# Channel sums taken from x as loaded, down products scaled into SBUF in one instruction, every offset on GpSimd, and new orders on all engines

## The chip, the cores and the metric

The kernel runs on one core of a Trainium2 chip. The time is device microseconds of one launch; 81.67 us is the median of three runs (81.64 to 82.47). Engines: TensorE (PE), VectorE (DVE), ScalarE (ACT), GpSimd (POOL), and SyncE (SP), which here only issues transfers. Every engine works through its own instructions in the order written and waits on semaphores.

## The reference

The input x is [64 batches, 64 tokens, 256 channels] in fp32, cond is [64, 128]. Two conditioned residual layers are applied:

```python
dg, db, ug, ub = (cond @ t for t in (down_gamma, down_beta, up_gamma, up_beta))
w_down = down_project[None] * dg[:, None] + db[:, None]          # [b, 256, 64]
act = relu(einsum('bsd,bdh->bsh', x, w_down))
w_up = up_project[None] * ug[:, None] + ub[:, None]              # [b, 64, 256]
x = x + (einsum('bsh,bhd->bsd', act, w_up) + x)                  # layer 0
styles = cond @ (affine_w * gain).T + affine_b
dcoefs = rsqrt(sum((weight * styles)**2) + 1e-8)
y = clip(einsum('blc,oc->blo', x * styles, weight) * dcoefs + bias, -256, 256)
x = x + y                                                        # layer 1
```

Since `db` is the same for all channels of one batch and one h, its share of the down product is `db` times the sum of x over the 256 channels of a token: the **channel sum**. Likewise `ub` needs the sum of `act` over h.

## The kernel before

The 4096 tokens are worked in eight tiles of 512 tokens (eight batches). For a tile t the stages are:

1. `transpose_in`: PE turns x (`x_nat`, tokens on partitions) into channels on partitions, in PSUM `ps_io`. ACT copies it to `hT` (`evacuate_x`).
2. `pair_x` (POOL, L582) adds the two halves of 128 channels of `hT` into `x_pair`.
3. `down_project` (PE, L713) and `down_sum` (PE, L720, ones times `x_pair`) fill the two halves of `ps_down`: the product (g=0) and the channel sum spread over all h (g=1). Tokens 0 to 255 lie on partitions 0 to 63, the others on 64 to 127. Tile 1 uses a bank of `ps_y` for this, since `ps_down` holds the result up to `relu_low`.
4. `scale_down` (DVE, L374) multiplies each half by its table, g=1 into SBUF `sum_sc`, g=0 in place in PSUM. `sum_down` (L381) adds them in place in PSUM. `relu_high` (ACT) and `relu_low` (DVE, L386 and L388) write the rounded relu and its rest to `act_hl`.
5. `up` (PE, L733 to L735): up product in `ps_up`, sum over h in `ps_sum`. `scale_up` and `add_up` (DVE, L394 and L407) make `hT` = scaled up product + `hT`. `evacuate_sum` (ACT) copies `ps_sum`; POOL's `offset_scale` (L588) and `offset_add` (L597) add the `ub` share to `hT`. For tile 4 DVE does the scaling itself (`OFFSET_ON_DVE`, L401).
6. `modulate` (POOL, L603): `xm` = `hT` times styles.
7. `linear(t, o)` (PE, L745): the second layer for output half o. Half 0 is demodulated and clipped below on ACT (`demodulate`, 8 instructions, L262), half 1 on DVE (L412, L417) for the tiles of `DEMOD_ON_DVE` and on ACT for tiles 0 and 2. `finish` (DVE, L423) clips above and adds `hT`.
8. `transpose_out` (PE, L699) and `evacuate_out` (ACT, L271), then the store by SP.

The last tile is done in two parts of 256 tokens and two output halves (`end_...`), so that its end is short. Tables (`down_tables`, `up_tables`, `styles`), the transposed weight (`transpose_weight`, L806) and the norms (`norms`, L816, with a root on ACT and one Newton step on DVE) are made in the first 27 us. The order of the work on each engine is a list of calls written out by hand at the end of that engine's block. SP issues all loads first, x tile 0 in four blocks, then tables, tile 1, more tables, the weight, tiles 2 to 7; after that the stores in order, each behind its wait.

Of the kernel before, what the change touches and what calls it, by code (L numbers as in the profile page):

```python
# [5 lines left out]
ALU = mybir.AluOpType  # L6
ACT = mybir.ActivationFunctionType
F32 = mybir.dt.float32
F32R = mybir.dt.float32r

P = 128
# [4 lines left out]
def bass_cond_resid(nc, x, cond, down_project, down_gamma, down_beta, up_project, up_gamma, up_beta,  # L16
# [19 lines left out]
    DEMOD_ON_DVE = (1, 3, 4, 5, 6)  # L36
    OFFSET_ON_DVE = (4,)
# [5 lines left out]
    with ExitStack() as ctx:  # L43
# [42 lines left out]
        sum_sc = sb("sum_sc", [P, HT])  # L86
# [32 lines left out]
        x_paired = sem("x_paired")  # L119
        down_ps, down_scaled, pre_ready = sem("down_ps"), sem("down_scaled"), sem("pre_ready")  # L120
        hi_ready, lo_ready = sem("hi_ready"), sem("lo_ready")
        up_ps, up_scaled, up_added = sem("up_ps"), sem("up_scaled"), sem("up_added")
        act_sum_ready, off_scaled, dve_off_scaled = sem("act_sum_ready"), sem("off_scaled"), sem("dve_off_scaled")
# [18 lines left out]
        def sums_before(t):  # L142

            return sum(n not in OFFSET_ON_DVE for n in range(t))

# [15 lines left out]

        def down_bank(t):

            return ps_y[:, 0].rearrange("p (g t) -> p g t", g=2) if t == 1 else ps_down[:]
# [21 lines left out]
        def _(sp):  # L186
# [13 lines left out]
            def store(n):  # L200
                parts = 1 if n < HALVED else 2
                for part in range(parts):
                    blocks = slice(part * TJ // parts, (part + 1) * TJ // parts)
                    sp.wait_ge(out_ready, outs_before(n) + part + 1)
                    sp.dma_start(out_tiles[n][:, blocks], out_nat[:, n, blocks]).then_inc(out_stored, 16)
# [6 lines left out]
            store(0)  # L212
            store(1)
            store(2)
            store(3)
            store(4)
            store(5)
            end_store(0, 0)
            store(6)
            end_store(0, 1)  # L220
            end_store(1, 0)
            end_store(1, 1)
# [3 lines left out]
        def _(act):  # L226
# [17 lines left out]

            def relu_high(t):
                act.wait_ge(pre_ready, t + 1)
                wait(act, up_ps, t - 1)
                q, pre = t % 2, down_bank(t)[:, 0]
                act.activation(act_hl[0:H, q, 0:HT], pre[0:H], ACT.Relu)
                act.activation(act_hl[H:P, q, HT:T], pre[H:P], ACT.Relu).then_inc(hi_ready, 1)  # L250

            def evacuate_sum(t):
                act.wait_ge(up_ps, t + 1)
                copied = [n for n in range(t) if n not in OFFSET_ON_DVE]
                wait(act, off_scaled, len(copied) - 1)
                act.activation(act_sum[:, len(copied) % 2], ps_sum[:], ACT.Copy).then_inc(act_sum_ready, 1)  # L256
# [70 lines left out]
            evacuate_sum(2)
            relu_high(3)
# [3 lines left out]
            relu_high(4)  # L332
            evacuate_sum(3)
            evacuate_x(6)
            demodulate(1, 0)
            evacuate_x(7)
            relu_high(5)
            demodulate(2, 1)
            demodulate(2, 0)
            evacuate_out(0)  # L340
            relu_high(6)
            evacuate_sum(5)
            evacuate_out(1)
            demodulate(3, 0)
            evacuate_out(2)
            evacuate_sum(6)
            relu_high(7)
            demodulate(4, 0)
            evacuate_out(3)
            evacuate_sum(7)  # L350
            demodulate(5, 0)
            evacuate_out(4)
            demodulate(6, 0)
            evacuate_out(5)
            evacuate_end(0, 0)
            evacuate_out(6)
            evacuate_end(0, 1)
            evacuate_end(1, 0)
            evacuate_end(1, 1)

        @block.vector
        def _(dve):
# [5 lines left out]

            def scale_down(t):
                dve.wait_ge(down_ps, t + 1)  # L370
                wait(dve, pre_ready, t)
                for g, scaled in ((1, sum_sc[:]), (0, down_bank(t)[:, 0])):
                    tab = down_tab[:, t, g].unsqueeze(2).to_broadcast([P, HB, S])
                    last = dve.tensor_tensor(scaled.rearrange("p (b s) -> p b s", s=S),  # L374
                                             down_bank(t)[:, g].rearrange("p (b s) -> p b s", s=S), tab, ALU.mult)
                last.then_inc(down_scaled, 1)

            def sum_down(t):
                dve.wait_ge(down_scaled, t + 1)
                pre = down_bank(t)[:, 0]  # L380
                dve.tensor_tensor(pre, pre, sum_sc[:], ALU.add).then_inc(pre_ready, 1)  # L381

            def relu_low(t):
                dve.wait_ge(hi_ready, t + 1)
                q, pre = t % 2, down_bank(t)[:, 0]
                dve.scalar_tensor_tensor(out=act_hl[H:P, q, 0:HT], in0=pre[0:H], scalar=0.0,  # L386
                                         in1=act_hl[0:H, q, 0:HT].bitcast(F32), op0=ALU.max, op1=ALU.subtract)
                dve.scalar_tensor_tensor(out=act_hl[0:H, q, HT:T], in0=pre[H:P], scalar=0.0,  # L388
# [7 lines left out]

            def offset_scale(t):
                dve.wait_ge(up_ps, t + 1)
                wait(dve, x2_ready, t - 1)
                sums = by_batch(ps_sum[:].unsqueeze(1).to_broadcast([P, DC, T]))  # L400
                dve.tensor_tensor(by_batch(off_sc[:, t % 2]), sums, per_batch(up_tab[:, 1, :, batches(t)]),  # L401
                                  ALU.mult).then_inc(dve_off_scaled, 1)
# [78 lines left out]

            down_tables()
            dve.wait_ge(dtab_sb, 1)
            scale_down(0)
            sum_down(0)
            up_tables()
            relu_low(0)
            scale_down(1)
            sum_down(1)
            dve.wait_ge(utab_sb, 1)  # L490
            scale_up(0)
            relu_low(1)
# [442 lines left out]
```

## Time and profile before

| | |
|---|---|
| three runs, median | 81.67 us |
| profiled execution, its own time | 82.11 us |
| its span | 80.2 us |
| granted TensorE clock | 1.00 (2.4 GHz) throughout |
| busy in the span: PE, DVE, ACT, POOL | 73.5, 60.1, 53.9, 58.9 us |
| loads, stores | 5.15 MB read, 4.19 MB written |

The span runs from the first to the last instruction of the profiled execution; its own time is 1.9 us more. PE being busy 92% doesn't by itself say that it is the limit, because matmuls overlap one another in the records; the chain of waits and the timeline say where nothing but PE stood in the way. A stage in which PE and POOL are both busy all the time has two limits that have to be moved together.

### The profile page before, as it was taken

What the parts mean: (1) busy time and instruction counts of PE and PEld (TensorE: products, weight loads), DVE (VectorE), ACT (ScalarE), POOL (GpSimd) and SP (SyncE); (2) the same over time, 40 slices, a digit from 0 to 9 for tenths busy, and PEclk for the clock granted to TensorE, in tenths of its full rate; (3) what the DMA queues carried; (4) which work ended last, traced back from release to release, by engine and by line L of the source; (5) the groups of instructions that cost most, each with busy time, mean ns of one, the idle gap of its engine ahead of it and who ended that gap; (6) DMA issues with size and microseconds to landing.
All of it is one profiled execution on the core that took longest, in us unless ns stands there. A gap on an engine that the chain in (4) does not pass through costs nothing.

```text
span 80.2 us, 1233 instructions
## 1 busy us (share of the span) xinstructions
PE 73.5 (92%) x378; PEld 45.6 (57%) x378; DVE 60.1 (75%) x105; ACT 53.9 (67%) x131; POOL 58.9 (73%) x41
## 2 busy tenths in 40 slices
PE   4997899998989999999999999999999999999720
PEld 2573586757966536743753564638547464587500
DVE  1001078399799699899799969998999989979820
ACT  0362480876693689974957999569799495297830
POOL 3005360299989999999999999999799999990000
PEclk9999999999999999999999999999999999999999
DMA  1889999996000000000000001542330610702696
GB/s 17 240 222 297 280 272 356 348 349 190 1 0 0 0 0 4 0 0 4 0 0 8 0 0 65 196 167 94 135 126 0 229 36 0 261 0 91 212 328 161
DMA packets 10734, 9.42 MB, mean 117 GB/s; under 512 B 1060, under 2 KB 10728, under 8 KB 10728
## 3 DMA queue, kind: packets, MB, share of 16 engines
q1 hardware_dynamic: 10352, 9.24, 36.6%
q10 hardware_dynamic: 376, 0.10, 0.5%
q8 instruction: 3, 0.05, 0.3%
q14 instruction: 3, 0.02, 0.1%
HBM read 5.15 MB, written 4.19 MB: 116 GB/s over the span
## 4 chain that ended last, share of the span: by engine, by line
PE 76%; DMA 8%; SPq 7%; ACT 2%; DVE 2%; issue 2%
PE ps_y L745 26%; PE ps_io L699 8%; DMA x_nat<-in_x_dram 8%; PE ps_io L688 8%; PE ps_down L713 8%; PE ps_up L733 6%; PE ps_up L734 5%; PE ps_down L720 4%; PE ps_sum L735 2%; PE ps_y L756 2%; PE ps_up L756 2%; PE ps_sum L745 2%; PE ps_down L745 2%; SPq L188 2%; SPq L192 1%
## 5 line engine op out<-in xcount | busy, mean ns | idle before, releaser
L262 ACT ACTIVATE ps_y<-ps_y,vec_cols,demod 128x64 f32<-128x64 f32 x64 | 19.5, 401 | 4.9 <-PE ps_y L745 4.9
L745 PE MATMUL ps_y<-xm,wT 128*128 128x512 f32 x48 | 21.7, 592 | 0.0
L582 POOL TENSOR_TENSOR x_pair<-hT 128x512 f32<-128x512 f32 x8 | 10.2, 1276 | 9.8 <-ACT hT L237 5.4
L597 POOL TENSOR_TENSOR hT<-hT,off_sc 128x1024 f32<-128x1024 f32 x7 | 16.6, 2367 | 0.2
L745 PEld LDWEIGHTS ps_y<-xm,wT 128*128 128x128 f32 x48 | 9.0, 189 | 8.7 <-issue 8.1
L603 POOL TENSOR_TENSOR xm<-hT,style 128x1024 f32<-128x1024 f32 x7 | 13.3, 1904 | 0.3
L588 POOL TENSOR_TENSOR off_sc<-act_sum,up_tab 128x1024 f32<-128x1024 f32 x6 | 11.4, 1906 | 0.6 <-ACT act_sum L256 0.6
L394 DVE TENSOR_TENSOR ps_up<-ps_up,up_tab 128x1024 f32<-128x1024 f32 x8 | 9.8, 1227 | 2.0 <-PE ps_sum L735 1.8
L407 DVE TENSOR_TENSOR hT<-ps_up,hT 128x1024 f32<-128x1024 f32 x8 | 9.8, 1220 | 0.2
L271 ACT ACTIVATE out_nat<-ps_io,shift 128x1024 f32<-128x1024 f32 (+1 forms) x9 | 8.2, 934 | 2.2 <-PE ps_io L699 1.9
L243 ACT ACTIVATE hT<-ps_io 128x1024 f32<-128x1024 f32 x7 | 7.2, 1031 | 3.1 <-PE ps_io L688 3.1
L423 DVE SCALAR_TENSOR_TENSOR z<-ps_y,hT 128x512 f32<-128x512 f32 x12 | 8.2, 685 | 0.7 <-ACT ps_y L262 0.5
L688 PE MATMUL ps_io<-ident,x_nat 128*128 128x128 f32 x56 | 7.5, 278 | 1.0 <-DMA x_nat<-in_x_dram 0.6
L688 PEld LDWEIGHTS ps_io<-ident,x_nat 128*128 128x128 f32 x56 | 6.1, 140 | 3.3 <-issue 1.7
L699 PEld LDWEIGHTS ps_io<-ident,z 128*128 128x128 f32 x56 | 6.3, 141 | 2.9 <-issue 2.8
L713 PE MATMUL ps_down<-hT,dp_sb 128*64 128x256 f32 x56 | 7.6, 392 | 0.3 <-ACT hT L237 0.3
L699 PE MATMUL ps_io<-ident,z 128*128 128x128 f32 x56 | 7.4, 275 | 0.1
L733 PE MATMUL ps_up<-act_hl,up_hi 128*128 128x512 f32 x16 | 7.0, 440 | 0.2 <-DVE hT L407 0.2
L374 DVE TENSOR_TENSOR sum_sc<-ps_down,down_tab 128x256 f32<-128x256 f32 x7 | 2.9, 419 | 4.6 <-PE ps_down L720 4.6
L734 PE MATMUL ps_up<-act_hl,up_lo 128*128 128x512 f32 x16 | 6.3, 395 | 0.0
L713 PEld LDWEIGHTS ps_down<-hT,dp_sb 128*64 128x64 f32 x56 | 3.4, 136 | 4.8 <-issue 3.4
L256 ACT ACTIVATE act_sum<-ps_sum 128x512 f32<-128x512 f32 x7 | 4.2, 600 | 2.0 <-PE ps_sum L735 1.8
(106 smaller groups left out, 108.9 us busy)
## 6 DMA issues: line engine op xcount, KB each, us to landing
x_nat<-in_x_dram SPq DMA_DIRECT2D x7, 512.0 KB, 8.3
out_dram<-out_nat SPq DMA_DIRECT2D x5, 512.0 KB, 2.9
out_dram<-out_nat SPq DMA_DIRECT2D x4, 256.0 KB, 2.8
x_nat<-in_x_dram SPq DMA_DIRECT2D x4, 128.0 KB, 2.7
out_dram<-out_nat SPq DMA_DIRECT2D x4, 128.0 KB, 2.4
w_sb<-in_L_cond_weight_dram SPq DMA_DIRECT2D x1, 256.0 KB, 5.0
up_sb<-n_L_cond_up_project_dram SPq DMA_DIRECT2D x2, 64.0 KB, 4.3
aff_sb<-in_L_cond_affine_w_dram SPq DMA_DIRECT2D x1, 128.0 KB, 4.3
```

Of the source, the lines that this page charges most:

```text
L262: last = act.activation(tokens, tokens, ACT.Relu, bias=vec_cols[:, DC + c:DC + c + 1], scale=demod[:, c, t * TB + b:t * TB + b + 1])
L394: dve.tensor_tensor(by_batch(ps_up[:]), by_batch(ps_up[:]), per_batch(up_tab[:, 0, :, batches(t)]), ALU.mult).then_inc(up_scaled, 1)
L582: pool.tensor_tensor(x_pair[:, t % 2], hT[:, t, 0], hT[:, t, 1], ALU.add).then_inc(x_paired, 1)
L588: pool.tensor_tensor(by_batch(off_sc[:, t % 2]), sums, per_batch(up_tab[:, 1, :, batches(t)]), ALU.mult).then_inc(off_scaled, 1)
L597: pool.tensor_tensor(hT[:, t], hT[:, t], off_sc[:, t % 2], ALU.add).then_inc(x2_ready, 1)
L603: pool.tensor_tensor(by_batch(xm[:, t % 3]), by_batch(hT[:, t]), per_batch(style2[:, :, batches(t)]), ALU.mult).then_inc(xm_ready, 1)
L688: last = pe.transpose(ps_io[:, c * T + j * P:c * T + (j + 1) * P], x_nat[:, t, j, c * P:(c + 1) * P], ident[:])
L699: last = pe.transpose(ps_io[:, j * D + c * P:j * D + (c + 1) * P], z[:, t % 3, c, j * P:(j + 1) * P], ident[:])
L713: pe.matmul(down_bank(t)[half * H:(half + 1) * H, 0], dp_sb[:, c], hT[:, t, c, halves(half)], start=(c == 0), stop=(c == DC - 1))
L733: pe.matmul(ps_up[:, c], up_hi[:, c * P:(c + 1) * P], act_hl[:, t % 2], start=True, stop=False)
L734: pe.matmul(ps_up[:, c], up_lo[:, c * P:(c + 1) * P], act_hl[:, t % 2], start=False, stop=True)
L745: last = pe.matmul(y_bank(t, o), wT[:, c, o * P:(o + 1) * P], xm[:, t % 3, c], start=(c == 0), stop=(c == DC - 1))
```

## The change

Channel sums. For seven tiles they are no longer made from `hT`. DVE (tiles 0, 1, 2: `sum_first`, `sum_tokens`) or ACT (tiles 3, 4, 6, 7: `sum_tokens`, four copies with an accumulator output; the copied values go to `out_nat` and are overwritten later) sums each token's 256 channels from `x_nat` as loaded. POOL's `spread` copies these four numbers per partition to `x_wide`, each 64 times, and PE's `down_sum_by_token` transposes two 128x128 blocks of it into the g=1 half of `ps_down`. Tile 5 (`PAIRED`) keeps `pair_x` and the product with ones.

Down products. `scale_down` is one instruction over both halves, from PSUM to SBUF `down_sc`; `sum_down` adds the two halves of it into SBUF `pre`, and the relu instructions read `pre`. `ps_down` is free once it has been scaled.

Offsets. POOL scales the offset of tile 4 too; `OFFSET_ON_DVE` and its semaphore go. Half 1 of tile 2 is demodulated on DVE.

Orders. All five lists are new. The stores of tiles 5 and 6 are issued in halves between those of the last tile.

```diff
-    DEMOD_ON_DVE = (1, 3, 4, 5, 6)
-    OFFSET_ON_DVE = (4,)
+    DEMOD_ON_DVE = (1, 2, 3, 4, 5, 6)
+    PAIRED = (5,)
...
+            def sum_tokens(t):                                   # ACT
+                act.wait_ge(x_loaded[t], 16)
+                for j in range(TJ):
+                    act.activation(out_nat[:, t, j], x_nat[:, t, j], ACT.Copy,
+                                   accum_out=x_sum[:, t, j:j + 1]).then_inc(x_summed[t], 1)
...
+            def sum_tokens(t):                                   # DVE
+                dve.wait_ge(x_loaded[t], 16)
+                dve.tensor_reduce(x_sum[:, t], x_nat[:, t], AX.X, ALU.add).then_inc(x_summed[t], TJ)
...
             def scale_down(t):
                 dve.wait_ge(down_ps, t + 1)
+                dve.wait_ge(x_sum_ps, t + 1)
                 wait(dve, pre_ready, t)
-                for g, scaled in ((1, sum_sc[:]), (0, down_bank(t)[:, 0])):
...
+                dve.tensor_tensor(down_sc[:].rearrange("p g (b s) -> p (g b) s", s=S),
+                                  ps_down[:].rearrange("p g (b s) -> p (g b) s", s=S), tab,
+                                  ALU.mult).then_inc(down_scaled, 1)
             def sum_down(t):
                 dve.wait_ge(down_scaled, t + 1)
-                pre = down_bank(t)[:, 0]
-                dve.tensor_tensor(pre, pre, sum_sc[:], ALU.add).then_inc(pre_ready, 1)
+                wait(dve, lo_ready, t - 1)
+                dve.tensor_tensor(pre[:, t % 2], down_sc[:, 0], down_sc[:, 1], ALU.add).then_inc(pre_ready, 1)
...
+            def spread(t):                                       # POOL
+                k = spreads_before(t)
+                pool.wait_ge(x_summed[t], TJ)
+                if k > 1:
+                    pool.wait_ge(x_sum_ps, [n for n in range(t) if n not in PAIRED][k - 2] + 1)
+                both = x_sum[:, t].rearrange("p (h j) -> p j h", h=2).unsqueeze(3).to_broadcast([P, TJ // 2, 2, H])
+                pool.tensor_copy(x_wide[:, k % 2], both).then_inc(x_spread, 1)
...
             def down_project(t):                                 # PE
-                elif t > 1:
-                    pe.wait_ge(lo_ready, 1 if t == 2 else t)
+                wait(pe, down_scaled, t)
...
+            def down_sum_by_token(t):
+                pe.wait_ge(x_spread, spreads_before(t) + 1)
+                wait(pe, down_scaled, t)
+                for j in range(TJ // 2):
+                    last = pe.transpose(ps_down[:, 1, j * P:(j + 1) * P],
+                                        x_wide[:, spreads_before(t) % 2, j].rearrange("p h m -> p (h m)"), ident[:])
+                last.then_inc(x_sum_ps, 1)
...
             def transpose_weight():
                 pe.wait_ge(w_in, 16)
-                pe.wait_ge(lo_ready, 2)
```

PE, from the tables to the first `up` (the product of tile 1, then `transpose_in` of tile 2), before:

```order
L789 MATMUL ps_y<-condT,ugb_sb 128x64 x4
L713 MATMUL ps_y<-hT,dp_sb 64x256 x4
L720 MATMUL ps_y<-x_pair,ones 64x256 x2
L688 MATMUL ps_io<-ident,x_nat 128x128 x8
L733 MATMUL ps_up<-act_hl,up_hi 128x512
```

The same place in the changed kernel:

```order
L839 MATMUL ps_y<-condT,ugb_sb 128x64 x4
L763 MATMUL ps_down<-ident,x_wide 128x128 x2
L855 MATMUL ps_y<-ident,w_sb 128x128 x4
L754 MATMUL ps_down<-hT,dp_sb 64x256 x4
L726 MATMUL ps_io<-ident,x_nat 128x128 x8
```

The channel sum of tile 1 now stands ahead of its product, and the four transposes of the weight, which before stood behind the channel sum of tile 2, stand ahead of the transposes of tile 2.

PE at the end, from the first part's products of the last tile (L756, then L806), before:

```order
L756 MATMUL ps_up<-xm,wT 128x256 x2
L699 MATMUL ps_io<-ident,z 128x128 x8
L756 MATMUL ps_up<-xm,wT 128x256 x2
L764 MATMUL ps_up<-ident,z 128x128 x2
L756 MATMUL ps_y<-xm,wT 128x256 x2
L699 MATMUL ps_io<-ident,z 128x128 x8
L756 MATMUL ps_y<-xm,wT 128x256 x2
L764 MATMUL ps_up<-ident,z 128x128 x2
L764 MATMUL ps_y<-ident,z 128x128 x4
```

and now:

```order
L806 MATMUL ps_up<-xm,wT 128x256 x4
L737 MATMUL ps_io<-ident,z 128x128 x8
L814 MATMUL ps_up<-ident,z 128x128 x2
L806 MATMUL ps_y<-xm,wT 128x256 x4
L814 MATMUL ps_up<-ident,z 128x128 x2
L737 MATMUL ps_io<-ident,z 128x128 x8
L814 MATMUL ps_y<-ident,z 128x128 x4
```

The output transposes of tile 6 no longer stand between the last two products, but behind both.

DVE around the down stage of tile 2, before (the rows before the up product is scaled, and the two relu rests):

```order
L374 TENSOR_TENSOR sum_sc<-ps_down,down_tab 128x256
L374 TENSOR_TENSOR ps_down<-ps_down,down_tab 128x256
L381 TENSOR_TENSOR ps_down<-ps_down,sum_sc 128x256
L394 TENSOR_TENSOR ps_up<-ps_up,up_tab 128x1024
L386 SCALAR_TENSOR_TENSOR act_hl<-ps_down,act_hl 64x256
L388 SCALAR_TENSOR_TENSOR act_hl<-ps_down,act_hl 64x256
```

and now, from the scaling of tile 2 on:

```order
L403 TENSOR_TENSOR down_sc<-ps_down,down_tab 128x512
L410 TENSOR_TENSOR pre<-down_sc 128x256
L476 RECIPROCAL dm_r<-ps_y 128x128
L423 TENSOR_TENSOR ps_up<-ps_up,up_tab 128x1024
L429 TENSOR_TENSOR hT<-ps_up,hT 128x1024
L415 SCALAR_TENSOR_TENSOR act_hl<-pre,act_hl 64x256
L417 SCALAR_TENSOR_TENSOR act_hl<-pre,act_hl 64x256
```

`add_up` (L429) now runs right behind `scale_up`, ahead of the relu rests. The addition and both relu rests read two SBUF operands, where each of them read one from PSUM before.

## Rows read from the trace of the kernel before

**Rows 1.** The page: busy us, share of the span, instructions of an engine.

```profile
PE 73.5 (92%) x378; PEld 45.6 (57%) x378; DVE 60.1 (75%) x105; ACT 53.9 (67%) x131; POOL 58.9 (73%) x41
```

**Rows 2.** Busy time in a stretch: stretch, us, then each engine, clock, DMA, GB/s.

```profile
24.00:72.20 48.20, 48.20 (x219) 27.64 (x216) 43.86 (x70) 36.65 (x96) 46.81 (x27) 1.00 0.16 55
```

**Rows 3.** Chain of waits in order of time: start us, us, what.

```profile
6.40 0.43 SPq L196
...
6.88 6.31 DMA x_nat<-in_x_dram
...
13.23 1.09 PE ps_io L688 x8
...
16.60 1.01 PE ps_down L713 x8
17.61 0.43 PE ps_down L720 x4
18.04 0.59 PE ps_y L806 x4
...
72.26 0.22 PE ps_up L764 x2
```

**Rows 4.** Timeline of PE, where it stood idle: start, us, instruction [idle before].

```profile
19.22 0.47 PE L733 MATMUL ps_up<-act_hl,up_hi 128*128 128x512 f32 x1 [0.20 <-DVE hT L407]
...
22.70 1.06 PE L688 MATMUL ps_io<-ident,x_nat 128*128 128x128 f32 x8 [0.36 <-ACT hT L243]
```

**Rows 5.** Groups of POOL: count | busy us, mean ns | idle before.

```profile
L597 POOL TENSOR_TENSOR hT<-hT,off_sc 128x1024 f32<-128x1024 f32 x7 | 16.6, 2367 | 0.2
L603 POOL TENSOR_TENSOR xm<-hT,style 128x1024 f32<-128x1024 f32 x7 | 13.3, 1904 | 0.3
L588 POOL TENSOR_TENSOR off_sc<-act_sum,up_tab 128x1024 f32<-128x1024 f32 x6 | 11.4, 1906 | 0.6 <-ACT act_sum L256 0.6
L582 POOL TENSOR_TENSOR x_pair<-hT 128x512 f32<-128x512 f32 x8 | 10.2, 1276 | 9.8 <-ACT hT L237 5.4 <-ACT hT L243 4.4
...
L631 POOL TENSOR_TENSOR up_lo<-up_sb,up_hi 128x256 fp32r<-128x256 f32 x1 | 0.7, 732 | 1.2 <-ACT up_hi L309 1.2
```

**Rows 6.** Timeline of POOL: first offset, two idle times, last instruction.

```profile
16.80 1.90 POOL L588 TENSOR_TENSOR off_sc<-act_sum,up_tab 128x1024 f32<-128x1024 f32 x1
...
22.64 1.27 POOL L582 TENSOR_TENSOR x_pair<-hT 128x512 f32<-128x512 f32 x1 [0.36 <-ACT hT L243]
...
57.14 1.90 POOL L588 TENSOR_TENSOR off_sc<-act_sum,up_tab 128x1024 f32<-128x1024 f32 x1 [0.57 <-ACT act_sum L256]
...
71.12 1.04 POOL L626 TENSOR_TENSOR xm<-hT,style 128x512 f32<-128x512 f32 x1
```

**Rows 7.** Groups of DVE, by size.

```profile
L407 DVE TENSOR_TENSOR hT<-ps_up,hT 128x1024 f32<-128x1024 f32 x8 | 9.8, 1220 | 0.2
...
L374 DVE TENSOR_TENSOR sum_sc<-ps_down,down_tab 128x256 f32<-128x256 f32 x7 | 2.9, 419 | 4.6 <-PE ps_down L720 4.6
...
L412 DVE TENSOR_TENSOR ps_y<-ps_y,demod 128x512 f32<-128x512 f32 x4 | 2.8, 699 | 0.4 <-PE ps_y L745 0.2
```

**Rows 8.** Groups of ACT, by size.

```profile
L262 ACT ACTIVATE ps_y<-ps_y,vec_cols,demod 128x64 f32<-128x64 f32 x64 | 19.5, 401 | 4.9 <-PE ps_y L745 4.9
...
L309 ACT ACTIVATE up_hi<-up_sb 128x256 fp32r<-128x256 f32 x1 | 0.4, 418 | 2.1 <-DMA up_sb<-n_L_cond_up_project_dram 2.1
...
L306 ACT ACTIVATE condT<-ps_sum 128x64 f32<-128x64 f32 x1 | 0.2, 216 | 0.0
```

**Rows 9.** Timeline of the end, all engines.

```profile
72.31 1.04 PE L756 MATMUL ps_y<-xm,wT 128*128 128x256 f32 x4
...
73.43 1.06 PE L699 MATMUL ps_io<-ident,z 128*128 128x128 f32 x8
...
77.34 0.47 ACT L277 ACTIVATE out_nat<-ps_y,shift 128x256 f32<-128x256 f32 x1 [0.82 <-PE ps_y L764]
```

**Rows 10.** DMA issues: count, KB each, median us from issue to landing.

```profile
w_sb<-in_L_cond_weight_dram SPq DMA_DIRECT2D x1, 256.0 KB, 5.0
```

More of the change, by code:

```diff
@@ L140, in wait, with spreads_before @@
                 eng.wait_ge(s, count)
-        def sums_before(t):
-            return sum(n not in OFFSET_ON_DVE for n in range(t))
+        def spreads_before(t):
+            return sum(n not in PAIRED for n in range(t))
         def outs_before(t):
@@ L198, in _, with store @@
                 sp.dma_start(x_nat[:, n], x_tiles[n]).then_inc(x_loaded[n], 16)
-            def store(n):
+            def store(n, part):
                 parts = 1 if n < HALVED else 2
[L202 to L205, printed above, removed]
+                blocks = slice(part * TJ // parts, (part + 1) * TJ // parts)
+                sp.wait_ge(out_ready, outs_before(n) + part + 1)
+                sp.dma_start(out_tiles[n][:, blocks], out_nat[:, n, blocks]).then_inc(out_stored, 16)
             def end_store(part, o):
@@ L505, in _ @@
             newton_result()
-            relu_low(3)
             scale_up(2)
             add_up(2)
+            relu_low(3)
+            scale_down(4)
             finish(0, 1)
-            scale_down(4)
             sum_down(4)
+            scale_up(3)
             finish(0, 0)
-            scale_up(3)
             relu_low(4)
+            add_up(3)
             dve.wait_ge(newton, 4)
@@ L517, in _ @@
             clip_low(1)
-            add_up(3)
+            scale_down(5)
             finish(1, 1)
-            scale_down(5)
+            scale_up(4)
             finish(1, 0)
             sum_down(5)
-            scale_up(4)
+            add_up(4)
+            demodulate(2)
+            clip_low(2)
             relu_low(5)
-            offset_scale(4)
-            add_up(4)
+            scale_down(6)
             finish(2, 1)
-            scale_down(6)
             sum_down(6)
@@ L531, in _ @@
             scale_up(5)
+            scale_down(7)
+            add_up(5)
+            sum_down(7)
+            relu_low(6)
             demodulate(3)
-            relu_low(6)
+            finish(3, 0)
             clip_low(3)
-            add_up(5)
+            scale_up(6)
             finish(3, 1)
-            scale_down(7)
-            finish(3, 0)
-            sum_down(7)
-            scale_up(6)
+            add_up(6)
             relu_low(7)
-            add_up(6)
+            finish(4, 0)
             demodulate(4)
-            finish(4, 0)
             clip_low(4)
@@ L862, in _ @@
             linear(0, 1)
+            up(2)
+            down_sum_by_token(4)
+            down_project(4)
             pe.wait_ge(wT_sb, 1)
```

290 lines of the change are left out of this document (152 added, 138 removed).

## The prediction, made before the changed kernel was run

> **What bounds the kernel now.** The page first: PE is busy 92% of the span, DVE 75%, POOL 73% [rows 1]. These are averages, so the stretches come next: from 24.0 to 72.2 us PE has no idle time at all, POOL is busy 46.81 of 48.20 us and DVE 43.86 [rows 2]. The chain of waits says what holds each stage: up to 13.2 us it is the loads, ending with x tile 2, which the transposes of tile 2 wait for; from 13.23 us on the chain is almost wholly PE, to the last output transposes [rows 3]. PE stood idle in that part only twice by more than 0.1 us, 0.20 us for `add_up` of tile 0 and 0.36 us for the copy of tile 4 [rows 4]. POOL's own queue runs nearly without a gap from the first offset at 16.80 us to the last `modulate`, which ends at 72.16 [rows 6]; the product that needs it starts on PE at 72.31 [rows 9]. So two engines arrive together: less work on PE alone would have ended in a wait for POOL. The change must shorten both.
>
> **PE.** The product with ones costs 0.43 us of the chain, a pair of 128x128 transposes of data of the same kind 0.22 [rows 3]. Behind 13.23 us lie the sums of tiles 2, 3, 4, 6 and 7 (tile 5 keeps the old way, tiles 0 and 1 lie in the time of the loads): 5 x 0.21 = **1.05 us**. The weight's transposes, 0.59 us at 18.04 [rows 3], move ahead of the transposes of tile 2. Their load is issued at 6.40 and takes 5.0 us, or up to 5.4 with its issue [rows 3, 10]: 11.4 to 11.8, so they end at about 12.4, and the 1.01 us of `down_project` [rows 3] behind them at 13.4, where 13.23 was the start of tile 2. That gives 0.2 back: **0.4 us**. The two idle times [rows 4] go, since `add_up` of tile 0 now runs ahead of the relu rest and PE has norms and a down product between, and since the copy of tile 4 has `up`, a product and a sum before the next user of its bank: **0.55 us**. Together 2.0 us.
>
> **POOL.** From 16.80 on it ran five pair additions (tiles 3 to 7). Four go, four spreads come, and one offset scaling comes: -4 x 1.28 + 4 x s + 1.91 [rows 5]. The trace has no broadcast copy of 256 elements. Above, it is bounded by the two-input one of that size, 0.73; below, by a quarter of the 512-wide addition's time, 0.3 [rows 5]. I take s = 0.5, midway, since one input is read and not two. That is -1.2 us; the idle 0.36 us for the copy of tile 5 goes with its pair addition's later place, and the 0.57 us for a copied sum [rows 6] should go as the sums are ready earlier than POOL. In all -2.1 us (bounds -1.2 and -2.9). It is as much as PE's 2.0, so neither is left waiting long. Per tile POOL's work stands behind `evacuate_sum` and `add_up`, which both move up with PE.
>
> **DVE.** `scale_down` was two instructions of 0.42, now one of 512 columns, like the 0.70 of `demodulate` [rows 7]: -0.14 for each of eight. The offset of tile 4 goes (1024 wide, like the 1.22 row), half 1 of tile 2 comes (0.70 for the scaling and as much for the clip of that width). Net -0.9 us. The reductions (four of 256, two of 1024) cost between half and the whole of the two-input rows, 0.42 and 1.22 [rows 7]; I take the whole, 4.1 us. They lie before 15.5 us: POOL and DVE are idle there waiting for the first pair sum (4.6 us on DVE alone, [rows 7]), and the first scaling comes 1.5 to 2 us earlier, because its sum no longer waits for `hT` and POOL. The last, of tile 2, stands ahead of `scale_up` of tile 0, which needs `up` at about 15.6 anyway. So nothing on the path; if `up` were earlier, that reduction would be late next.
>
> **ACT.** Sixteen copies of 256 with an accumulator output: nearest is the plain 256 copy from SBUF, 0.42 us; above, I add a small instruction of 0.22 for reading the accumulator, 0.64 [rows 8]. I take 0.42: 6.7 us. One more sum copy (0.6), and eight instructions of 0.31 to 0.40 fewer (`demodulate(2, 1)`), -2.5 to -3.2 [rows 8]. Some 4.5 us on an engine that had 26 us free [rows 1]. Queued behind the sums: the root (now ready early), `evacuate_sum` of tile 3 and the copy of x tile 6, all used by PE some 1 us later. The nearest of them: walking along the new lists with these durations, the sum of tile 3 is copied at about 35.5, and `up` of tile 4, which waits for it, comes up on PE at 36.6. Their cover is that 1 us.
>
> **The end.** From the start of the last part's products at 72.31 to the end of the last copy at 77.81 are 5.5 us [rows 9]. The transposes of tile 6 (1.06 us at 73.43, the next product overlapping the last of it) leave the path between the two products: some 0.9 us. But ACT then has two halves of tile 6 in turn with the last copies and ends at about 5.05, and a 256 KB store goes out just ahead of the last one. Of 0.45 us I count **0.2**.
>
> **Sum:** 1.05 + 0.4 + 0.55 + 0.2 = 2.2 us. The profiled execution had a span of 80.2 and a time of its own of 82.11, so it would be 78.0 and 79.9; it stands 0.44 above the median, so on the median 81.67 - 2.2 = 79.4 us.
>
> **A price that the trace doesn't hold.** Before, every DVE instruction here with two tensor inputs had one in PSUM, and POOL's durations don't vary beside them: the 1024-wide additions mean 2.37 us each, the products 1.90 [rows 5]. Now `sum_down` and both relu rests read two operands from SBUF, 18 times in tiles 2 to 7, while POOL is 97% busy [rows 2]. No row shows such a pair of instructions at once. One end is nothing; the other is that one of the two engines stands still for the whole instruction of the other.
> The Trainium skill, SBUF — State Buffer, section Who interferes with whom, says just this: a VectorE instruction with two SBUF inputs and a GpSimd instruction that reads SBUF take turns under an exclusive lock, whichever started first. By that rule the sum would change sign; what no trace here shows I leave as a rival.
>
> **Rivals.**
> 1. *VectorE and GpSimd block each other* (slower). If DVE waits for the running POOL instruction: with 2.37, 1.90 and 1.90 back to back the mean rest is (5.6 + 3.6 + 3.6) / (2 x 6.17) = 1.04 us; two waits a tile (the relu pair counted as one), six tiles, 12.5 us. DVE has 4.3 us free between 24.0 and 72.2 [rows 2], so 8.2 us come on top: 87.6 us. If POOL waits instead, 18 x 0.42 = 7.6 us on a queue without slack: 87.0 us. The place is POOL's queue from tile 2 on; it decides from 2.2 / 18 = 0.12 us a piece on. A part of that price, a third to two thirds, gives 82 to 85. For it: both operands are new in SBUF and POOL is always running. Against: POOL's durations here are indifferent to DVE, which reads SBUF beside it all the time, if with one operand. Chance 0.14 for the whole, 0.12 for a part.
> 2. *ACT late* (no change). At 0.64 us a copy the sums of tiles 3, 4 and 6 put ACT 2.6 us later; less the 1 us of cover, PE waits about 1.5 us for the sum copy of tile 3 and the x copy of tile 6: 80.9 us. The same result comes if POOL's spread costs its upper bound and PE waits for `modulate`: 80.3. Chance 0.12 that it ends within 1%.
> 3. *The sums don't shorten PE.* That would need a transpose pair as long as 0.43; [rows 3] has the pair at 0.22, so this is inside the forecast's range.
>
> **Numbers.** The forecast, chance 0.62: 79.4, its own range 78.5 (bounds of spread and end in favour, whole 0.45 of the end) to 80.8. Runs of this kernel tell about 1% from no change, 0.8 us. Faster by over 1% 0.62, within 1% 0.12, slower 0.26. For 8 in 10 the upper end must reach into the first rival, leaving its whole price out: 78.5 to 86.0.
>
> **What would show it.** Right: `down_sum_by_token` 0.22 on PE, transposes of tile 2 at 13.2 to 13.5, PE without idle time from there on, POOL's last `modulate` ending near 70.0, no wait of PE for `modulate`. Wrong: POOL instructions longer than 2.4 and 1.9 us, or DVE standing idle ahead of `sum_down` and the relu rests, or these longer than 0.42 (rival 1); copies with accumulator over 0.5 us and PE waiting for ACT (rival 2). The forecast fails most easily on the queue of DVE, 91% busy in that stretch: any new wait there reaches PE through `add_up` and `finish`.

## The result, and the profile after

The changed kernel takes **94.69 us** (median of 4 runs, 94.16 to 95.49) where the kernel before takes 81.66 (4 runs beside it, 81.61 to 82.47): a ratio of 1.158, 95% interval 1.146 to 1.169. Forecast were 79.4 us and a range up to 86.0, so both the sign and the range are wrong. What came is rival 1, and dearer than I priced it. The profiled execution has a span of 93.1 us, 12.9 more than before. Some executions of the kernels below ran in a slower state of the chip; the ratios leave them out, so a ratio and a pair of medians can differ.

The page of the changed kernel, busy us, share of the span and instructions, then PE's granted clock in 40 slices; the first row stands against [rows 1]:

```profile
PE 74.8 (80%) x364; PEld 46.9 (50%) x364; DVE 77.8 (84%) x104; ACT 58.7 (63%) x156; POOL 57.4 (62%) x42
...
PEclk9999999999999996699999999995799999999985
```

DVE has one instruction fewer and 17.7 us more of busy time. So something made its instructions longer. The groups of DVE in the changed kernel, by size (count | busy us, mean ns of one | idle before), say which:

```profile
L417 DVE SCALAR_TENSOR_TENSOR act_hl<-pre,act_hl 64x256 fp32r<-64x256 f32 x8 | 11.3, 1419 | 0.1
...
L429 DVE TENSOR_TENSOR hT<-ps_up,hT 128x1024 f32<-128x1024 f32 x8 | 9.8, 1220 | 0.2
L410 DVE TENSOR_TENSOR pre<-down_sc 128x256 f32<-128x256 f32 x8 | 8.2, 1022 | 0.1
...
L415 DVE SCALAR_TENSOR_TENSOR act_hl<-pre,act_hl 64x256 fp32r<-64x256 f32 x8 | 5.7, 719 | 0.3
```

`sum_down` (L410) and the two halves of `relu_low` (L415, L417) are the instructions that now read two tensors from SBUF. `add_up` (L429), which reads one from PSUM and one from SBUF, still takes the 1.22 us of [rows 7]. The lengthened time counts as busy, not as idle: a reader who looks only for waits does not find it.

Two stretches of the timeline of the changed kernel show where it comes from. First DVE (start us, us, instruction):

```profile
18.65 2.49 DVE L417 SCALAR_TENSOR_TENSOR act_hl<-pre,act_hl 64x256 fp32r<-64x256 f32 x1
...
32.45 0.79 DVE L415 SCALAR_TENSOR_TENSOR act_hl<-pre,act_hl 64x256 fp32r<-64x256 f32 x1
33.25 2.03 DVE L417 SCALAR_TENSOR_TENSOR act_hl<-pre,act_hl 64x256 fp32r<-64x256 f32 x1
...
39.59 0.42 DVE L415 SCALAR_TENSOR_TENSOR act_hl<-pre,act_hl 64x256 fp32r<-64x256 f32 x1
40.03 0.42 DVE L417 SCALAR_TENSOR_TENSOR act_hl<-pre,act_hl 64x256 fp32r<-64x256 f32 x1
...
58.64 2.01 DVE L415 SCALAR_TENSOR_TENSOR act_hl<-pre,act_hl 64x256 fp32r<-64x256 f32 x1
60.66 2.47 DVE L417 SCALAR_TENSOR_TENSOR act_hl<-pre,act_hl 64x256 fp32r<-64x256 f32 x1
```

Then POOL in the same places, also of the changed kernel:

```profile
18.35 2.51 POOL L631 TENSOR_TENSOR hT<-hT,off_sc 128x1024 f32<-128x1024 f32 x1
...
31.06 1.90 POOL L625 TENSOR_TENSOR off_sc<-act_sum,up_tab 128x1024 f32<-128x1024 f32 x1 [0.45 <-ACT act_sum L263]
32.92 2.08 POOL L637 TENSOR_TENSOR xm<-hT,style 128x1024 f32<-128x1024 f32 x1
...
37.60 1.97 POOL L637 TENSOR_TENSOR xm<-hT,style 128x1024 f32<-128x1024 f32 x1
40.97 1.90 POOL L625 TENSOR_TENSOR off_sc<-act_sum,up_tab 128x1024 f32<-128x1024 f32 x1 [1.40 <-ACT act_sum L263]
...
58.29 2.08 POOL L637 TENSOR_TENSOR xm<-hT,style 128x1024 f32<-128x1024 f32 x1
60.34 2.52 POOL L631 TENSOR_TENSOR hT<-hT,off_sc 128x1024 f32<-128x1024 f32 x1
```

Each long DVE instruction ends 0.27 to 0.28 us after the POOL instruction it met: 35.28 and 35.00, 21.14 and 20.86, 60.65 and 60.37, 63.13 and 62.86. For the others of these three lines that took 0.5 us or more it is 0.27 to 0.29. Where POOL stands idle, from 39.57 to 40.97, the same two instructions take 0.42 each. The Trainium skill (SBUF — State Buffer, section Who interferes with whom) calls the pair of ports that the two engines share an exclusive lock, which a VectorE instruction with two SBUF inputs and a GpSimd instruction that reads SBUF contend for. The rows above agree.

DVE's queue hands the delay on. The waits of PE in the changed kernel (us in total, times, longest), and its timeline behind the two relu rests of 33.25 and 60.66:

```profile
PE ps_up L782 <- issue: 10.4, 6, 3.7
```

```profile
35.38 0.62 PE L782 MATMUL ps_up<-act_hl,up_hi 128*128 128x512 f32 x1 [2.43 <-issue]
...
63.23 0.76 PE L782 MATMUL ps_up<-act_hl,up_hi 128*128 128x512 f32 x1 [3.70 <-issue]
```

"issue" hides the releaser, but the ends tell it: PE starts `up` 0.10 us after each of the two rests ends (35.28, 63.13). In the stretch from 24.0 us to the start of the last part's products, the sums close. The first row is the changed kernel's, the second, in a fence of its own, that of the kernel before:

```profile
24.00:84.41 60.41, 50.80 (x211) 29.61 (x210) 57.71 (x68) 40.04 (x114) 48.06 (x29) 0.94 0.13 44
```

```profile
24.00:72.31 48.31, 48.31 (x220) 27.75 (x217) 43.97 (x70) 36.76 (x96) 46.81 (x27) 1.00 0.16 55
```

The stretch is 12.10 us longer. DVE, the third engine in the row, is busy 13.74 us more and idle 1.64 us less (2.70 instead of 4.34), and 13.74 - 1.64 = 12.10. PE, busy throughout before, is idle 9.61 us. POOL is idle 12.35 us instead of 1.50. DVE sets the pace.

### The profile page after: what moved, and what is told of

Same layout as the page of the kernel before. It is cut to its first block, busy times and chain, and to the rows that moved or that the text cites. A ratio compares the mean times of both kernels' runs of the same rounds, so it can differ in the third digit from the quotient of the medians.

```text
span 93.1 us, 1244 instructions
## 1 busy us (share of the span) xinstructions
PE 74.8 (80%) x364; PEld 46.9 (50%) x364; DVE 77.8 (84%) x104; ACT 58.7 (63%) x156; POOL 57.4 (62%) x42
## 4 chain that ended last, share of the span: by engine, by line
PE 68%; issue 11%; DMA 7%; SPq 6%; ACT 3%; ACTq 0%
PE ps_y L795 23%; PE ps_down L754 7%; DMA x_nat<-in_x_dram 7%; PE ps_io L737 7%; PE ps_up L782 6%; PE ps_io L726 6%; PE ps_up L783 5%; PE ps_sum L784 2%; PE ps_y L806 2%; PE ps_up L806 2%; PE ps_sum L795 2%; PE ps_down L795 2%; SPq L189 2%; ACT out_nat L277 1%; PE ps_down L763 1%
## 5 line engine op out<-in xcount | busy, mean ns | idle before, releaser
L795 PE MATMUL ps_y<-xm,wT 128*128 128x512 f32 x48 | 22.9, 606 | 0.5 <-issue 0.4
L269 ACT ACTIVATE ps_y<-ps_y,vec_cols,demod 128x64 f32<-128x64 f32 x56 | 17.0, 394 | 3.9 <-PE ps_y L795 3.9
L631 POOL TENSOR_TENSOR hT<-hT,off_sc 128x1024 f32<-128x1024 f32 x7 | 17.6, 2510 | 0.6 <-DVE hT L429 0.5
L782 PE MATMUL ps_up<-act_hl,up_hi 128*128 128x512 f32 x16 | 8.2, 512 | 10.4 <-issue 10.4
L625 POOL TENSOR_TENSOR off_sc<-act_sum,up_tab 128x1024 f32<-128x1024 f32 x7 | 13.3, 1900 | 4.9 <-ACT act_sum L263 4.9
L417 DVE SCALAR_TENSOR_TENSOR act_hl<-pre,act_hl 64x256 fp32r<-64x256 f32 x8 | 11.3, 1419 | 0.1
L612 POOL COPY x_wide<-x_sum 128x256 f32<-128x256 f32 x7 | 3.3, 478 | 12.0 <-DVE x_sum L396 5.0
L782 PEld LDWEIGHTS ps_up<-act_hl,up_hi 128*128 128x128 f32 x16 | 3.4, 212 | 13.5 <-issue 13.1
L429 DVE TENSOR_TENSOR hT<-ps_up,hT 128x1024 f32<-128x1024 f32 x8 | 9.8, 1220 | 0.2
L754 PE MATMUL ps_down<-hT,dp_sb 128*64 128x256 f32 x64 | 9.3, 415 | 0.0
L410 DVE TENSOR_TENSOR pre<-down_sc 128x256 f32<-128x256 f32 x8 | 8.2, 1022 | 0.1
L403 DVE TENSOR_TENSOR down_sc<-ps_down,down_tab 128x512 f32<-128x512 f32 x8 | 5.5, 688 | 3.1 <-PE ps_down L754 3.0
```

Of the source, the lines that this page charges most:

```text
L269: last = act.activation(tokens, tokens, ACT.Relu, bias=vec_cols[:, DC + c:DC + c + 1], scale=demod[:, c, t * TB + b:t * TB + b + 1])
L429: dve.tensor_tensor(hT[:, t], ps_up[:], hT[:, t], ALU.add).then_inc(up_added, 1)
L625: pool.tensor_tensor(by_batch(off_sc[:, t % 2]), sums, per_batch(up_tab[:, 1, :, batches(t)]), ALU.mult).then_inc(off_scaled, 1)
L631: pool.tensor_tensor(hT[:, t], hT[:, t], off_sc[:, t % 2], ALU.add).then_inc(x2_ready, 1)
L754: last = pe.matmul(ps_down[half * H:(half + 1) * H, 0], dp_sb[:, c], hT[:, t, c, halves(half)], start=(c == 0), stop=(c == DC - 1))
L782: pe.matmul(ps_up[:, c], up_hi[:, c * P:(c + 1) * P], act_hl[:, t % 2], start=True, stop=False)
```

## The experiments

Runs beside a kernel stand against the runs of the kernel before on the same chip; these had medians of 82.27 us (first four experiments), 82.62 (e5 and e6) and 82.39 (e7, e8). In the edits, `...` stands for lines left out.

**e1_sum_two_sbuf**, the kernel before with one operand moved:

```diff
+        prod_sc = sb("prod_sc", [P, HT])
-                for g, scaled in ((1, sum_sc[:]), (0, down_bank(t)[:, 0])):
+                for g, scaled in ((1, sum_sc[:]), (0, prod_sc[:])):
-                dve.tensor_tensor(pre, pre, sum_sc[:], ALU.add).then_inc(pre_ready, 1)
+                dve.tensor_tensor(pre, prod_sc[:], sum_sc[:], ALU.add).then_inc(pre_ready, 1)
```

> The kernel before, with one thing of the change: the scaled product goes to SBUF too, so sum_down reads two SBUF operands (and still writes its sum to PSUM). Orders, channel sums and all other instructions are those of before. Theory L (a VectorE instruction with two SBUF operands waits for the end of the GpSimd instruction that runs): in the changed kernel sum_down took 8.2 us for eight instead of 3.4, 0.6 us more each; here six of them stand beside a running GpSimd, 3.6 to 6 us more on VectorE, of which 4.3 us lie in its free time at best: 82.5 to 86 us, with sum_down rows of 1 to 2.5 us. Theory O (the new orders and ScalarE's sums cost the time, not the operands): 81.7 us and sum_down at 0.43.

Measured: 84.2 us, ratio 1.026 (1.017 to 1.035). Its groups of DVE:

```profile
L382 DVE TENSOR_TENSOR ps_down<-prod_sc,sum_sc 128x256 f32<-128x256 f32 x7 | 9.1, 1299 | 0.2
L389 DVE SCALAR_TENSOR_TENSOR act_hl<-ps_down,act_hl 64x256 fp32r<-64x256 f32 x7 | 3.0, 426 | 0.1
L387 DVE SCALAR_TENSOR_TENSOR act_hl<-ps_down,act_hl 64x256 fp32r<-64x256 f32 x7 | 2.9, 417 | 1.0 <-ACT act_hl L251 0.8
...
L375 DVE TENSOR_TENSOR prod_sc<-ps_down,down_tab 128x256 f32<-128x256 f32 x7 | 2.9, 415 | 0.0
...
L382 DVE TENSOR_TENSOR ps_y<-prod_sc,sum_sc 128x256 f32<-128x256 f32 x1 | 0.4, 434 | 0.0
```

Only the instruction with two SBUF operands grew, by 0.88 us each, 6.2 in all; the product that writes SBUF and the relu rests, still fed from PSUM, did not. The delay needs both, two SBUF operands and a POOL at work: the sum of tile 1, in the last row, ran at 15.94 us while POOL was idle and took 0.43. So the place of one operand, beside a running POOL, is the cause. And 6.2 us cost only 2.1 on the ratio: here most of DVE's slack of 4.3 us could be used.

**e2_down_in_sbuf**, the kernel before with the down part alone as in the change (one scaling into SBUF, sum and relu from there), old channel sums, old orders:

```diff
-        sum_sc = sb("sum_sc", [P, HT])
+        down_sc = sb("down_sc", [P, 2, HT])
+        pre_sb = sb("pre_sb", [P, 2, HT])
...
-                q, pre = t % 2, down_bank(t)[:, 0]
+                q, pre = t % 2, pre_sb[:, t % 2]
```

> The kernel before with the whole down part of the change and nothing else: one scaling into SBUF, sum_down from SBUF to SBUF, both relu parts from SBUF; the old orders, pair sums and offsets. Theory L: 18 exposed instructions, as in the changed kernel, some 15 us more of VectorE time, so 91 to 98 us, and granted clock below 1 where PE waits. Theory O: 81 to 82 us. If it comes near 86, the operands are half of the loss and the orders the other half.

Measured: 97.62 us, ratio 1.190 (1.178 to 1.201). The sum and the relu rests:

```profile
L381 DVE TENSOR_TENSOR pre_sb<-down_sc 128x256 f32<-128x256 f32 x8 | 10.9, 1361 | 0.2
L388 DVE SCALAR_TENSOR_TENSOR act_hl<-pre_sb,act_hl 64x256 fp32r<-64x256 f32 x8 | 10.8, 1346 | 0.1
...
L386 DVE SCALAR_TENSOR_TENSOR act_hl<-pre_sb,act_hl 64x256 fp32r<-64x256 f32 x8 | 7.0, 875 | 1.2 <-ACT act_hl L251 0.9
```

The down part alone costs more than the whole change, so the rest of the change gives some 2.6 us back (by the ratios, 1.190 and 1.158). These three lines are busy 28.7 us here against 25.2 in the changed kernel. So what comes back may well be time not spent waiting for POOL, which has the pair additions here, and not the gains that I forecast; the two were not separated.

**e3_token_sums_psum**, the other half: channel sums from x as loaded (seven tiles), the down part in PSUM and the orders as before, offset of tile 4 on DVE:

```diff
+        x_sum = sb("x_sum", [P, TILES, TJ])
+        x_wide = sb("x_wide", [P, 2, TJ // 2, 2, H])
...
-            pair_x(0)
+            spread(0)
```

> The other half: channel sums of seven tiles from x as loaded (VectorE 0 to 2, ScalarE 3, 4, 6, 7), spread on GpSimd and transposes on PE, tile 5 in pairs, but the down products scaled, added and read in PSUM as before, and before's orders with the new pieces put in; the offset of tile 4 stays on VectorE and the weight's transposes where they were. No VectorE instruction has two SBUF operands. Theory L: PE saves 5 x 0.21 us and GpSimd 5 us, nothing waits: 79.8 to 81.2 us, VectorE rows of the down stage at 0.42 to 0.43. Theory O: ScalarE's 4 x 1.7 us of sums delay what stands behind them, 82 to 85 us.

Measured: 82.03 us, ratio 0.996 (0.991 to 1.001). A miss: no gain that can be told from none, though the interval leaves room for 0.9%, where five sums at 0.21 us would be 1.3%. All DVE rows of the down part are at 0.42 to 0.43 us. PE's timeline in its profiled execution shows where time went:

```profile
14.22 0.44 PE L765 MATMUL ps_y<-ident,x_wide 128*128 128x128 f32 x2 [0.56 <-POOL x_wide L616]
14.50 1.04 PE L727 MATMUL ps_io<-ident,x_nat 128*128 128x128 f32 x8
```

The channel sum of tile 1 waited for POOL's spread, and the transposes of tile 2 began at 14.50 instead of 13.23. From the first linear product (27.78) to the start of `end_linear(1, 0)` (73.10) are 45.32 us instead of 45.90 before. So the three sums behind it gave their 3 x 0.2 us, and the loss lies ahead of it; how much of it the other executions share is not on record.

**e4_sum_from_psum**, the changed kernel with the sum fed from PSUM again, the relu rests still from SBUF:

```diff
-                dve.tensor_tensor(pre[:, t % 2], down_sc[:, 0], down_sc[:, 1], ALU.add).then_inc(pre_ready, 1)
+                dve.tensor_tensor(pre[:, t % 2], ps_down[:, 0], down_sc[:, 1], ALU.add).then_inc(pre_ready, 1)
```

> The changed kernel with one thing taken back: the product half is scaled in place in PSUM (two scalings), so sum_down reads one PSUM and one SBUF operand; the relu parts still read two SBUF operands; PE's next down product waits for sum_down instead of the scaling. Theory L: the 4.8 us that sum_down had too much go, less 0.1 us a tile for the second scaling: 88.5 to 92 us, sum_down at 0.43, relu rests as long as in the changed kernel. Theory O: 94 to 96 us.

Measured: 91.44 us median, 88.72 to 92.54 in 4 runs, too spread for a ratio; the mean granted clock was 0.988 in the fastest and 0.941 to 0.974 in the others. The sum's row:

```profile
L411 DVE TENSOR_TENSOR pre<-ps_down,down_sc 128x256 f32<-128x256 f32 x8 | 3.3, 417 | 0.1
```

The sum fell from 1022 to 417 ns, the rests stayed at 736 and 1378. Of the 13.0 us of the change the median gives 3.3 back and the fastest run 6.0. So the two rests carry half of the loss or more; four runs so far apart don't say it closer.

**e6_split_pool**, the changed kernel with each 1024-wide POOL instruction of tiles 0 to 6 as two of 512, the same arithmetic:

```diff
-                pool.tensor_tensor(hT[:, t], hT[:, t], off_sc[:, t % 2], ALU.add).then_inc(x2_ready, 1)
+                for c in range(DC):
+                    last = pool.tensor_tensor(hT[:, t, c], hT[:, t, c], off_sc[:, t % 2, c], ALU.add)
+                last.then_inc(x2_ready, 1)
```

> The changed kernel with GpSimd's offset scalings, offset additions and modulations of tiles 0 to 6 each as two instructions of 512 columns instead of one of 1024; VectorE, ScalarE and PE unchanged. GpSimd's own work grows by some 0.3 us a tile (2 x 1.27 for 2.37, 2 x 1.04 for 1.90). Theory L with the lock held for a whole instruction: the rest of the running instruction halves, the relu rests and sum_down fall from 1.42, 0.72 and 1.02 us to about 0.9, 0.55 and 0.7, 4 to 8 us less VectorE time and 87 to 92 us. Theory S (both engines share the interface by bandwidth): the VectorE rows stay as long, and with more GpSimd work the time is 94 to 97 us.

Measured: 87.82 us, ratio to before 1.067 (1.057 to 1.076), about 7 us under the changed kernel. Its groups of DVE, then of POOL:

```profile
L417 DVE SCALAR_TENSOR_TENSOR act_hl<-pre,act_hl 64x256 fp32r<-64x256 f32 x8 | 7.7, 958 | 0.1
L415 DVE SCALAR_TENSOR_TENSOR act_hl<-pre,act_hl 64x256 fp32r<-64x256 f32 x8 | 6.2, 772 | 0.3
L410 DVE TENSOR_TENSOR pre<-down_sc 128x256 f32<-128x256 f32 x8 | 5.6, 698 | 0.1
```

```profile
L634 POOL TENSOR_TENSOR hT<-hT,off_sc 128x512 f32<-128x512 f32 x14 | 18.8, 1363 | 0.2
L642 POOL TENSOR_TENSOR xm<-hT,style 128x512 f32<-128x512 f32 x14 | 15.3, 1111 | 0.2
L626 POOL TENSOR_TENSOR off_sc<-act_sum,up_tab 128x512 f32<-128x512 f32 x14 | 14.9, 1081 | 0.2 <-ACT act_sum L263 0.2
```

POOL's three groups take 49.0 us instead of 45.2, and yet the kernel is faster. Sharing of bandwidth would not depend on where an instruction ends; a wait for the whole POOL instruction does. The timeline says it too: the rest of 19.61 ends at 21.03, 0.29 us after the first half of the addition (19.39 to 20.74), while the second half runs to 22.17. How much of the 7 us is waiting and how much the clock is taken up under "Left open".

**e5_psum_new_start** asks what the rest of the change is worth without the lock: down part in PSUM, channel sums, early weight transposes, new start and end:

```diff
-            down_project(1)
             down_sum(1)
+            transpose_weight()
+            down_project(1)
...
+            evacuate_out(6, 0)
             evacuate_end(1, 0)
+            evacuate_out(6, 1)
             evacuate_end(1, 1)
```

> A version without any VectorE instruction of two SBUF operands that takes over what the change gained elsewhere: token sums for seven tiles, the weight's transposes ahead of those of tile 2, sum ahead of product in the down stage, the changed kernel's end order; down stage in PSUM (one bank, held up to the relu rests), relu of tile 1 moved ahead of the up scaling, offset of tile 4 on VectorE. By the terms of the prediction: the weight's 0.6 us, 5 x 0.21 us of sums, some 0.5 us of idle time at the start, 0.2 to 0.45 at the end: 79.2 to 80.4 us. If those terms were wrong (the weight's place or the end gives nothing): 81 to 82 us, as the version with token sums alone.

Measured: 82.13 us, ratio 0.995 (0.989 to 1.001). A miss again. **e7_old_end** (its edit against e5) takes the end back, **e8_copy_first** (against e7) goes for the idle times at the start:

```diff
-            evacuate_out(5, 0)
+            evacuate_out(5)
             evacuate_end(0, 0)
-            evacuate_out(5, 1)
+            evacuate_out(6)
             evacuate_end(0, 1)
-            evacuate_out(6, 0)
             evacuate_end(1, 0)
-            evacuate_out(6, 1)
             evacuate_end(1, 1)
```

> The same kernel as e5_psum_new_start but with the end of the kernel before: tile 5 and tile 6 stored in the old order, the transposes of tile 6 between the two last products. Theory 1, the new end is a wash: in e5 the last part took 5.0 us to the last ACT copy instead of 5.5, but the last store ended 3.0 us behind that copy instead of 2.4. Then this kernel ends 5.5 + 2.4 = 7.9 us after its end_linear(1, 0) starts, against 8.0 in e5, and its time equals e5's, ratio to before 0.99 to 1.00. Theory 2, the new end is worth 0.4 us: ratio 1.000 to 1.005.

```diff
-    PAIRED = (5,)
+    PAIRED = (2, 5)
...
-            relu_high(1)
             evacuate_x(2)
+            relu_high(1)
...
-            sum_tokens(2)
             dve.wait_ge(utab_sb, 1)
-            relu_low(1)
             scale_up(0)
+            relu_low(1)
```

> As e7_old_end, and the three idle times of PE in e5 (0.70 at 15.3, 0.49 at 18.5, 0.36 at 22.1 us) attacked: ACT copies x tile 2 ahead of relu_high(1) and x tile 3 ahead of the styles, DVE scales up(0) ahead of relu_low(1), and tile 2 gets its channel sum by the old pair addition and the product with ones, so that the 1.21 us reduction of tile 2 leaves DVE's queue (PE pays 0.43 instead of 0.22). If those idle times are what e5 lost, up(1) starts about 0.7 us earlier than in e7 and up(2) 0.9, and the ratio to before is 0.98 to 0.99. If PE only meets the next wait (ACT's copy of tile 3 or 4, POOL's pair addition of tile 2 before down_sum(2)), the ratio is that of e7.

Measured: e7 82.69 us by the median of all its 12 runs against 82.39, but a ratio of 0.988 (0.983 to 0.994); e8 82.56, ratio 0.996 (0.990 to 1.003). PE's timeline in e7, then in e8:

```profile
13.16 1.09 PE L728 MATMUL ps_io<-ident,x_nat 128*128 128x128 f32 x8
...
16.51 1.06 PE L728 MATMUL ps_io<-ident,x_nat 128*128 128x128 f32 x8 [0.70 <-ACT hT L248]
...
19.30 0.47 PE L780 MATMUL ps_up<-act_hl,up_hi 128*128 128x512 f32 x1 [0.49 <-DVE hT L431]
...
22.77 1.07 PE L728 MATMUL ps_io<-ident,x_nat 128*128 128x128 f32 x8 [0.36 <-ACT hT L248]
```

```profile
13.57 1.09 PE L727 MATMUL ps_io<-ident,x_nat 128*128 128x128 f32 x8 [0.34 <-DMA x_nat<-in_x_dram]
...
16.06 1.04 PE L727 MATMUL ps_io<-ident,x_nat 128*128 128x128 f32 x8
...
18.12 0.65 PE L760 MATMUL ps_down<-x_pair,ones 128*64 128x256 f32 x4 [1.01 <-DVE act_hl L412]
...
19.57 0.49 PE L779 MATMUL ps_up<-act_hl,up_hi 128*128 128x512 f32 x1
...
23.07 1.06 PE L727 MATMUL ps_io<-ident,x_nat 128*128 128x128 f32 x8 [0.36 <-ACT hT L248]
```

e8 took away 0.70 and 0.49 and got 1.01 in their place: with the relu rest behind the scaling of `up`, the bank of the down part came free later. `up` of tile 1 starts at 19.57 instead of 19.30, but only because x tile 2 landed later in this execution: from the start of its transposes (13.57 and 13.16) to that `up` are 6.00 us instead of 6.14. So 0.14 came of the 0.7 us expected. For the end, e7 takes 7.75 us from the start of `end_linear(1, 0)` (71.55) to the end of its span (79.3), e5 8.0 (71.21 to 79.2), the kernel before 7.9: the new end is a wash.

## Why the prediction was wrong, step by step

**The step that failed** is "A price that the trace doesn't hold". I saw that three instructions a tile would read two SBUF operands beside a POOL that never rests, saw that 0.12 us each would decide, and still put the price at nothing in the sum and 0.26 on the rival, on the ground that POOL's durations are "indifferent to DVE, which reads SBUF beside it all the time, if with one operand". That ground was no evidence: it speaks of pairs with one operand in PSUM, and the new pair has none. e1 shows that the second operand is all the difference, e6 that the wait lasts until the POOL instruction ends. In place of nothing, the three lines cost 12.9 us more of DVE's time in the stretch from 24 us on.

**The rival's price.** The 12.5 us of DVE waits were right in their total, in part by luck. In the stretch of 60.41 us the three lines were busy 6.90 + 4.67 + 8.44 = 20.01 us in 17 instructions; at 0.42 each that would be 7.1, so the excess is 12.9. But the sums have 4.8 us of it, where I had 6.2, and the relu pairs 8.1, where I had 6.2. Wrong was also what I took off. The rival's sum was 8.2 - 2.2 = 6.0 us above the median; the spans differ by 12.9. The 6.9 between, by its parts (rounded):
- DVE's slack of 4.3 us: only 1.64 was used, 2.7 us less. Likely because the waits come in lumps of up to 2.07 us (2.49 for 0.42), behind which PE, ACT and POOL are late for DVE's next work.
- the gains of PE and POOL, 2.0 us, were taken off from a kernel that DVE sets the pace of. In this sum of DVE's busy and idle time they have no place.
- other work on DVE in the stretch, 13.74 - 12.9 = 0.9 us, for which the rival's sum had no term. In part it is only the place of the cut at 24.00: one more `scale_up` and one more relu pair lie behind it than before. The two widths of tile 2's demodulation are in it too, against one offset scaling less.
- the excess itself, 12.9 instead of 12.5: 0.4 us.
- the end: 93.1 - 84.41 = 8.7 us instead of 7.9, where I had -0.2: 1.0 us.

I had also counted the relu pair as one wait. The rows give each its own, in the mean of eight: `sum_down` 0.60 us over 0.42, the first rest 0.30, the second 1.00. The first rest gets through when POOL's instruction ends, the next POOL instruction takes its turn, and the second rest waits for all of that one.

**PE's terms.** The pair of transposes is 0.22 on PE (starts 47.00 and 47.22):

```profile
13.33 1.09 PE L726 MATMUL ps_io<-ident,x_nat 128*128 128x128 f32 x8 [0.40 <-DMA x_nat<-in_x_dram]
...
47.00 0.38 PE L763 MATMUL ps_down<-ident,x_wide 128*128 128x128 f32 x2
47.22 1.88 PE L795 MATMUL ps_y<-xm,wT 128*128 128x512 f32 x4
```

Tile 2's transposes started at 13.33, forecast 13.2 to 13.5, but that is luck. I had PE's own queue set the start; in fact PE was free at 12.93 and waited 0.40 us for the load of x tile 2. Before the first linear product PE had done by 24.73 the work that took until 25.14 before, 0.41 us less, with a new wait of 1.29 us for the first long rest (21.14) in it. So without that wait the start would have been worth 1.7 us, about the 1.4 that I had for it. By size those terms held. That DVE is the bound behind them is why they don't show in the time.

**Without the lock** they don't come in full either. In e5, at the start of `end_linear(1, 0)`, 71.21 against 72.31, PE is 1.1 us ahead, of forecast 2.0. The three sums behind the first linear product were worth what they should, 0.59 (45.31 us from it to `end_linear(1, 0)` instead of 45.90; 3 x 0.21 = 0.63). The start gave 0.5 instead of 1.4, and 0.4 of this is that the transposes of tile 2 began earlier:

```profile
12.83 1.09 PE L730 MATMUL ps_io<-ident,x_nat 128*128 128x128 f32 x8
```

From there to the first linear product (25.90) are 13.07 us instead of 13.18, with idle times of 0.70, 0.49 and 0.36 us against 0.20 and 0.36 [rows 4]. They eat up the saved work: PE only meets its next wait, for ACT's copy and for DVE's `add_up`. The change's start leans on a down part that leaves PSUM early and frees its bank; that very move brings the lock. Span and time differ too: e5's profiled execution has a span of 79.2 us and a time of its own of 81.57, 2.4 us more, where the kernel before had 1.9 more. Of 1.0 us in the span only 0.5 is in the time, and no run says why.

**POOL.** The spread is 0.40 us at its shortest, 0.48 in the mean; I took 0.5. Offset scalings stayed at 1.90 us, additions went from 2367 to 2510 ns and products from 1904 to 2043. POOL is slowed too, by 14 x 0.14 = 2.0 us, but this is hidden: it idles 12.35 us in the stretch.

**ACT.** The two rows of the sums in the changed kernel:

```profile
L250 ACT ACTIVATE out_nat<-x_nat 128x256 f32<-128x256 f32 x16 | 6.5, 404 | 0.1
...
L250 ACT ACTIVATION_READ_ACCUMULATOR out_nat<-x_nat 128x1 f32 x16 | 3.0, 186 | 0.0
```

The accumulator read is an instruction of its own, yet overlaps the copies: in e5 four pairs start 0.40 us apart (18.19, 18.59, 18.99, 19.39). My 0.42 held, rival 2 did not come. DVE's reductions took 0.42 and 1.21, as bounded.

**Rival 3** is out with the row of 0.22.

**Left open.** PE's granted clock, 1.00 throughout the stretch before, is 0.94 now. After the gaps of 2.43 and 3.70 us a 512-column product takes 0.63 us instead of 0.39 to 0.40: this is the lower of the two levels, 1.2 GHz. In the two parts from 35.38 to 43.0 and 63.23 to 67.6 the clock was 0.78 and 0.65, so PE lost about 7.62 x 0.22 + 4.37 x 0.35 = 3.2 us. How much of that reaches the end can't be told: DVE was nearly full there. In e6, with gaps of 1.8 us at most, the mean clock was 0.994, and part of its gain may be this. Whether e7 gains anything is open as well, since its median and its ratio point different ways; by its ratio it is 1.2%. No kernel here beats the one before beyond doubt.

## What to carry to other kernels

Before moving an operand of a VectorE instruction from PSUM to SBUF, count the GpSimd instructions that run beside it: each DVE instruction with two SBUF tensors may wait for a whole one of them, 2 us here for 0.42 us of work. A cost that no row shows is not at nothing when only a few hundredths of a microsecond each would turn the sign; try that pair of instructions first, as e1 does by moving one operand. If the operands must be in SBUF, shorter GpSimd instructions shorten the wait: in e6 they gave back 7 of 13 us. And when such a cost makes another engine the bound, the gains on the old bound must not be taken off its price.

## What the runs showed of the hardware

- A DVE instruction with two SBUF operands that met a running POOL instruction ended 0.27 to 0.29 us after it, whatever that one's length (0.4 to 2.6 us in the changed kernel). Where POOL was idle it took 0.42 us. The profile counts the whole time as busy.
- Of two such instructions in a row, the second waited for the next POOL instruction as a whole (33.25 to 35.28 after 32.45 to 33.24).
- Beside a running POOL the operand's place decides: the sum took 1299 ns with two in SBUF (e1) and 417 with one in PSUM (e4). Writing SBUF from PSUM stayed at 415 ns (e1).
- ACT's accumulator output added 186 ns of busy time to a copy of 256 columns, hidden by overlap: such copies start 0.40 us apart (e5).
- With two halves stored just ahead of the last piece, the span's end lay 3.7 us behind the last ACT copy (89.42) in the changed kernel and 3.0 in e5, against 2.4 before and 2.25 in e7.
